# Cross attention one pair shorter in flight, the copy of the turned x ahead of the latent rows, the latent variance first in a pair, a second row of identity transposes

## The chip, the cores and the metric

One core of a Trainium2 chip runs the whole program in one launch. Time is the device time of one execution in microseconds (us); the runs of the kernel before gave 1091.06, 1090.47 and 1090.14, median 1090.47. The engines run their own instruction streams and meet at semaphores: PE (TensorE: matrix products, and transposes as products with the identity), DVE (VectorE), ACT (ScalarE), POOL (GpSimd) and SP (SyncE, which issues most transfers). Each engine takes its instructions in the order in which they are written.

## The reference

Three parts follow each other, each adding to x (32 sequences of 64 rows of 512 numbers): a masked cross attention over 256 context rows, a latent attention (q and kv are first projected to 384 + 128 + 64 columns, normalised and rotated), and a feed-forward part. The change lies in the first part and in the projection to latent rows:

```
x = x + xattn(layernorm(x), ctx, mask)          # scores = xn @ ctx.T, softmax, @ ctx
h = layernorm(x)                                # the "second normalisation"
z = h @ [wq_a; wkv_a].T + bias                  # 576 columns: q 384, kv 128, rope 64
q, kv = rmsnorm(z[:384]), rmsnorm(z[384:512])   # one mean of squares for each
rope = z[512:] * cos + rotate_half(z[512:]) * sin
```

## The kernel before

`stage_x` handles the 2048 rows as 16 pairs of sequences of 128 rows each. One slot of the loop (`slot(p, par)`, p = 0 to 15, written once for each engine) works on several pairs at once. In slot p of the kernel before:

- PE: `score(p)` (one product that adds the mask, then 16 of 64x256), `read(p-1)` (probabilities times context rows, 8 products), `turn1(p-2)` (4 transposes of the second normalisation), `turn0(p+1)`, `project(p-3)` (24 products of 288 columns with the latent weights), `turn` of the probabilities of p.
- ACT: copy of the turned probabilities of p-1 (L417), first normalisation of p+1 (L395, out x_xn), `squares(p-4)` (two sums of squares, L422 and L424), `exp(p)` (L412), `scale_q(p-4)` (L429), `turned1_hi(p-2)` (L406), `turned0(p+1)` (L400), second normalisation of p-1 (L395 too), and the transfer of z of pair p-4.
- DVE: `maximum(p)` (L503), `first_var(p+2)` (L467, L471, L474), `latent_var(p-4)` (two small instructions at L486 that wait for the sums of squares), `residual(p-1)` (L517, then L467, L471, L476), `turned1_lo(p-2)` (L462), `validate(p)` (L507, L512), `latent_kv(p-4)` (L491), `bias(p-3)` (L531, two).
- POOL: `rstd_of(0, p+2)` (L347, L351), `latent_rstd(p-4)` (L357), `rotate(p-4)` (L364 to L369), `rstd_of(1, p-1)` (L347, L351); in slot 2 also the rounding of the latent weights `w_raw` to `w_hi` (L381), from which DVE makes `w_lo` (L462).
- SP: the loads of x (p+6), of the turned context (p+4) and of the context rows (p+3), held back only by their buffers.

Whether a pair's second normalisation can start is set by a chain over three engines: `residual` and its variance on DVE, `rstd_of(1, ...)` on POOL, L395 on ACT. Behind slot 15 (the handover, in `program`) the last pairs are drained by hand-written lists while `Weights` multiplies the attention's weights out: 12 `fill_keys` (L1303) and then `fill_values` (L1313) on PE, each in one of four banks, which ACT (`keys_hi`, L1323) and DVE (`keys_lo`, L1338) empty, and `rope_scaled`, `rope_hi`, `rope_lo` on POOL (L1359, L1364, L1368).

Of the kernel before, what the change touches and what calls it, by code (L numbers as in the profile page):

```python
# [182 lines left out]
def stage_x(nc, ctx, A, scratch, mem, banks, w):  # L183
# [76 lines left out]
    def sync(sp):  # L260
# [66 lines left out]
        sp.dma_start(small[:], A["small"]).then_inc(s["small_loaded"], 16)  # L327
# [60 lines left out]
    def scalar(act):  # L388
# [42 lines left out]
        def slot(p, par):  # L431
# [130 lines left out]
    def tensor(pe):  # L562
        t = nc.tensor

        def turn(dst, src, n=KH):
# [28 lines left out]
        def score(p):  # L594
# [1520 lines left out]
```

## Time and profile before

| | |
|---|---|
| profiled execution | 1090.33 us, span 1088.5 us |
| busy | PE 1063.1 us (98%), PEld 904.0 (83%), DVE 508.1 (47%), ACT 338.9 (31%), POOL 294.9 (27%) |
| chain that ended last | PE 95%, DVE 2%, issue 1%, DMA 1%, POOL 1% |
| PE, 40 slices of 27 us | 5999989999999999999999999999999999999997 |
| GB/s in the first seven slices | 359 414 418 394 404 230 87 |
| waits of PE up to 230 us | 6.9 us for the first normalisation (L395), 3.7 us for `keys_lo` (L1338), 2.4 us for the turned probabilities (L417), 1.7 us for the mask (L557), 1.0 us for `turned0` (L400) |

PE is busy in all slices but the first, the sixth (the handover) and the last. A line of the timeline is one instruction, or several that merged: start, duration, engine, line, what it writes from what it reads, and in brackets how long the engine had been idle and what ended that. Durations overlap, since an engine starts the next instruction before the last has left its pipeline; the distance between two starts is what an instruction holds its engine.

### The profile page before, as it was taken

To read this page: it belongs to the slowest core of one execution; us is meant where nothing else is said; L and a number is where in the kernel's file an instruction comes from. 1 tells how busy PE (TensorE), PEld (TensorE's weight loads), DVE (VectorE), ACT (ScalarE), POOL (GpSimd) and SP (SyncE) were. 2 spreads that over 40 slices of the span, in tenths; PEclk is the share of its full clock that TensorE was granted. 3 is DMA by queue.
4 is the path that set the end of the run, shared out by engine and by line. 5 is a ranking of instruction groups with operands and counts; after the bars stand their busy time and mean duration, and the time that the engine had idled before them with its cause. 6 is when DMAs were issued, how large, how long until landed. Compare 5 with 4: busy or idle time off the path is not lost.

```text
span 1088.5 us, 18667 instructions
## 1 busy us (share of the span) xinstructions
PE 1063.1 (98%) x7233; PEld 904.0 (83%) x7233; DVE 508.1 (47%) x914; ACT 338.9 (31%) x630; POOL 294.9 (27%) x341
## 2 busy tenths in 40 slices
PE   5999989999999999999999999999999999999997
PEld 3677777788888888888888888999999898989896
DVE  3666556545555554445455668532324232414232
ACT  3565554422222222223222236312222221313030
POOL 2434363321112101131112102423233232415050
PEclk9999999999999999999999999999999999999999
DMA  9999962200022000320012072200101010101000
GB/s 359 414 418 394 404 230 87 74 20 21 20 68 88 20 19 14 107 58 20 20 59 88 20 252 90 77 20 20 39 1 40 1 39 0 39 0 40 1 21 20
DMA packets 40851, 101.26 MB, mean 93 GB/s; under 512 B 7049, under 2 KB 11172, under 8 KB 36292
## 3 DMA queue, kind: packets, MB, share of 16 engines
q1 hardware_dynamic: 39044, 96.62, 24.9%
q10 hardware_dynamic: 1728, 3.54, 0.8%
q8 instruction: 55, 0.90, 0.3%
q14 instruction: 24, 0.20, 0.1%
HBM read 74.45 MB, written 17.30 MB: 84 GB/s over the span
## 4 chain that ended last, share of the span: by engine, by line
PE 95%; DVE 2%; issue 1%; DMA 1%; POOL 1%; ACT 0%; SPq 0%; POOLq 0%; DVEq 0%; ACTq 0%
PE b_z L44 6%; PE b_z L46 6%; PE b_z L45 6%; PE b_score L44 5%; PE b_score L46 5%; PE b_prob L46 5%; PE b_score L45 5%; PE b_prob L44 5%; PE b_prob L45 5%; PE b_turn L44 4%; PE b_turn L46 4%; PE b_turn L45 4%; PE b_read L46 4%; PE b_read L44 4%; PE b_read L45 4%; PE b_read L619 2%
## 5 line engine op out<-in xcount | busy, mean ns | idle before, releaser
L1505 POOL TENSOR_TENSOR f_hT_lo<-f_h,f_hT_hi 128x512 fp32r<-128x512 f32 x64 | 92.4, 1444 | 106.2 <-ACT f_hT_hi L1550 96.9
L812 POOL TENSOR_TENSOR m_sc<-m_sc,m_rs 128x1024 f32<-128x1024 f32 x16 | 30.5, 1905 | 241.9 <-DVE m_rs L975 241.9
L1606 DVE TENSOR_TENSOR f_h<-f_h 128x512 f32<-128x512 f32 x64 | 49.7, 777 | 91.4 <-ACT f_h L1545 91.1
L44 PE MATMUL b_z<-m_zT_lo,m_wq_hi 128*128 128x512 f32 x192 | 75.0, 390 | 1.0 <-issue 0.7
L45 PE MATMUL b_z<-m_zT_hi,m_wq_lo 128*128 128x512 f32 x192 | 74.7, 389 | 0.0
L46 PE MATMUL b_z<-m_zT_hi,m_wq_hi 128*128 128x512 f32 x192 | 74.7, 389 | 0.0
L44 PE MATMUL b_turn<-f_xnT_lo,f_up_hi 128*128 128x256 f32 x256 | 72.6, 283 | 0.0
L44 PE MATMUL b_read<-f_xnT_lo,f_up_hi 128*128 128x256 f32 x256 | 72.5, 283 | 0.0
L45 PE MATMUL b_read<-f_xnT_hi,f_up_lo 128*128 128x256 f32 x256 | 72.4, 283 | 0.0
L46 PE MATMUL b_read<-f_xnT_hi,f_up_hi 128*128 128x256 f32 x256 | 72.4, 283 | 0.0
L46 PE MATMUL b_turn<-f_xnT_hi,f_up_hi 128*128 128x256 f32 x256 | 72.4, 283 | 0.0
L45 PE MATMUL b_turn<-f_xnT_hi,f_up_lo 128*128 128x256 f32 x256 | 72.4, 283 | 0.0
L983 DVE TENSOR_TENSOR m_x<-b_score,m_x 128x512 f32<-128x512 f32 x32 | 22.1, 690 | 95.8 <-PE b_score L46 95.8
L854 ACT ACTIVATE m_qT<-b_z,m_q_bias 128x512 f32<-128x512 f32 x64 | 44.0, 689 | 70.5 <-PE b_z L46 64.7
L802 POOL TENSOR_TENSOR m_qpe<-m_qpe,m_swapped 128x512 f32<-128x512 f32 x32 | 41.2, 1289 | 79.1 <-DMA m_swapped<-m_by_sin 79.1
L1550 ACT CAST f_hT_hi<-f_h 128x512 fp32r<-128x512 f32 x64 | 39.8, 622 | 57.3 <-DVE f_h L1606 57.3
L1545 ACT ACTIVATE f_h<-b_turn 128x512 f32<-128x512 f32 x32 | 19.1, 598 | 112.8 <-PE b_turn L46 112.8
L1487 POOL TENSOR_TENSOR f_ve<-f_mv,m_eps 128x2 f32<-128x2 f32 x15 | 3.4, 226 | 182.9 <-DVE f_mv L1580 182.9
L875 ACT ACTIVATE m_sc<-m_sc 128x512 f32<-128x512 f32 x32 | 20.2, 632 | 104.8 <-DVE m_sc L967 104.8
L44 PE MATMUL b_score<-m_wvo_lo,m_oT_hi 128*128 128x512 f32 x128 | 51.4, 401 | 0.0
L44 PE MATMUL b_score<-f_down_lo,f_hT_hi 128*128 128x512 f32 x128 | 50.5, 394 | 0.3 <-issue 0.3
L44 PE MATMUL b_prob<-m_wvo_lo,m_oT_hi 128*128 128x512 f32 x128 | 50.6, 395 | 0.0
(268 smaller groups left out, 3098.7 us busy)
## 6 DMA issues: line engine op xcount, KB each, us to landing
x_ctx_in<-ctx_rows_dram SPq DMA_DIRECT2D x16, 1024.0 KB, 15.0
x_ctxT<-ctx_turned_dram SPq DMA_DIRECT2D x15, 1024.0 KB, 14.9
m_swapped<-m_by_sin SPq DMA_DIRECT2D x128, 64.0 KB, 2.0
m_raw<-attn_raw_dram SPq DMA_DIRECT2D x6, 768.0 KB, 10.6
m_z_in<-z_scratch SPq DMA_DIRECT2D x4, 1152.0 KB, 5.7
x_x_all<-x_dram SPq DMA_DIRECT2D x16, 256.0 KB, 15.7
m_x<-x_scratch SPq DMA_DIRECT2D x4, 1024.0 KB, 6.0
x_scratch<-m_x SPq DMA_DIRECT2D x4, 1024.0 KB, 4.7
```

What stands on the lines that cost most here:

```text
L44: nc.tensor.matmul(out, lh, rl, start=first, stop=False)
L45: nc.tensor.matmul(out, ll, rh, start=False, stop=False)
L46: return nc.tensor.matmul(out, lh, rh, start=False, stop=last)
L619: mm = t.matmul(b_read[rows], pT[:, c, rows], ctx_in[:, p % RING, chunks * b + c], start=c == 0, stop=c == chunks - 1)
L802: q.tensor_tensor(qpe[:, m], qpe[:, m], swapped[:], ALU.add).then_inc(s["qpe_done"], 1)
L812: q.tensor_tensor(e, e, rs[:].unsqueeze(2).broadcast_to([P, HB, SEQ]), ALU.mult).then_inc(s["normed"], 1)
L854: a.activation(qT[:, h], b_q[h % 2][:], ACT.Identity, bias=q_bias[:, HU * n + h:HU * n + h + 1]).then_inc(s["q_done"], 1)
L875: a.activation(sc[:, HALF * half:HALF * half + HALF], sc[:, HALF * half:HALF * half + HALF], ACT.Exp, scale=SCALE).then_inc(s["exped"], 1)
L983: v.tensor_tensor(x1[:, TILES[i]], b_w[i % 2][:], x1[:, TILES[i]], ALU.add).then_inc(s["x2_done"], 1)
L1505: g.tensor_tensor(hT_lo[:, 2 * n:2 * n + 2].rearrange("p m n -> p (m n)"), h[:, n % 2], hT_hi[:, 2 * n:2 * n + 2].bitcast(F32).rearrange(" ...
L1550: a.copy(hT_hi[:, 2 * n:2 * n + 2].rearrange("p m n -> p (m n)"), h[:, n % 2]).then_inc(s["h_hi"], 1)
L1606: v.tensor_tensor(h[:, n % 2], h[:, n % 2], h[:, n % 2], ALU.mult).then_inc(s["squared"], 1)
```

## The change

Every pair is projected one slot earlier: `project`, `squares`, `latent_var`, `latent_rstd`, `rotate`, `scale_q`, `latent_kv`, `bias` and the transfer of z take p-2 or p-3 where they took p-3 or p-4, and the hand-written lists behind slot 15 lose one pair. On PE `turn1(p-2)` goes ahead of `read(p-1)`. On ACT `turned1_hi(p-2)` goes ahead of `exp(p)`, and `scale_q` behind `turned0`. On DVE `latent_var` becomes the first instruction of a slot and `turned1_lo(p-2)` goes ahead of `first_var(p+2)`. The rounding of the latent weights moves from POOL in slot 2 to ACT in slot 1, and their load ahead of the turned context of pair 2. Two rows of 22 identity transposes are issued on PE, one ahead of everything and one at the start of slot 2; nothing reads what they write. In pair 0 the mask is added behind the products instead of ahead of them. The two `rope_scaled` of POOL move from behind slot 15 to the starts of slots 14 and 15.

```diff
@@ -313,22 +314,22 @@
         sp.dma_start(mask_u8[:], A["mask_BxS2_bk0"]).then_inc(s["masks_loaded"], 16)
         sp.wait_ge(s["pool_setup"], 2)
         sp.dma_start(picks[0:BATCH, 0:PAIRS].rearrange("p a n -> p (a n)"), A["picks"]).then_inc(s["masks_loaded"], 16)
+        load_ctxT(1)
         load_x(2)
-        load_ctxT(1)
         load_ctx(0)
         load_x(3)
+        sp.dma_start(w_raw[:], A["w_latent"].rearrange("(k p) n -> p k n", p=P)).then_inc(s["w_loaded"], 16)
         load_ctxT(2)
+        load_x(4)
         load_ctx(1)
-        load_x(4)
-        sp.dma_start(w_raw[:], A["w_latent"].rearrange("(k p) n -> p k n", p=P)).then_inc(s["w_loaded"], 16)
+        sp.dma_start(small[:], A["small"]).then_inc(s["small_loaded"], 16)
         load_ctxT(3)
         load_ctx(2)
         load_x(5)
-        sp.dma_start(small[:], A["small"]).then_inc(s["small_loaded"], 16)
         slots(slot)
         return dict(store_z=store_z, store_x1=store_x1)
 
-    def gpsimd(pool):
+    def gpsimd(pool, rope_scaled):
         g = nc.gpsimd
         held = pool.alloc_register("x_pool_held")
         g.memset(ident[:], 0.0).then_inc(s["pool_setup"], 1)
...
@@ -369,16 +370,15 @@
             g.tensor_tensor(zbuf[:, par, QLR + KVLR:ZW], rope_tmp[:, 0, :], rope_tmp[:, 1, :], ALU.add).then_inc(s["z_rope"], 1)
 
         def slot(p, par):
+            if p >= PAIRS - w.ROPE_ROUNDS:
+                rope_scaled(p - (PAIRS - w.ROPE_ROUNDS))
             if has(p + 2):
                 rstd_of(0, p + 2)
-            if has(p - 4):
-                latent_rstd(p - 4)
-                rotate(p - 4, par)
+            if has(p - 3):
+                latent_rstd(p - 3)
+                rotate(p - 3, 1 - par)
             if has(p - 1):
                 rstd_of(1, p - 1)
-            if p == 2:
-                pool.wait_ge(s["w_loaded"], 16)
-                g.tensor_copy(w_hi[:], w_raw[:]).then_inc(s["w_hi"], 1)
 
         rstd_of(0, 0)
         rstd_of(0, 1)
...
@@ -433,19 +433,22 @@
                 turned_probs(p - 1)
             if has(p + 1):
                 norm(0, p + 1, xn0, x_all[:, p + 1])
-            if has(p - 4):
-                squares(p - 4, par)
-            exp(p)
-            if has(p - 4):
-                scale_q(p - 4, par)
+            if has(p - 3):
+                squares(p - 3, 1 - par)
             if has(p - 2):
                 turned1_hi(p - 2, par)
+            exp(p)
             if has(p + 1):
                 turned0(p + 1)
+            if has(p - 3):
+                scale_q(p - 3, 1 - par)
             if has(p - 1):
                 norm(1, p - 1, xn1, x_all[:, p - 1])
-            if has(p - 4):
-                write_z(act, p - 4, par)
+            if p == 1:
+                act.wait_ge(s["w_loaded"], 16)
+                a.copy(w_hi[:].rearrange(flat), w_raw[:].rearrange(flat)).then_inc(s["w_hi"], 1)
+            if has(p - 3):
+                write_z(act, p - 3, 1 - par)
 
         norm(0, 0, xn0, x_all[:, 0])
         turned0(0)
...
@@ -531,23 +534,23 @@
                 v.tensor_tensor(zb[:, par, cols], b_z[n][:, 0:ZH], qkv_b[:, cols], ALU.add).then_inc(s["z_biased"], 1)
 
         def slot(p, par):
+            if has(p - 3):
+                latent_var(p - 3)
             maximum(p)
+            if has(p - 2):
+                turned1_lo(p - 2, par)
             if has(p + 2):
                 first_var(p + 2)
-            if has(p - 4):
-                latent_var(p - 4)
             if has(p - 1):
                 residual(p - 1)
+            validate(p)
+            if has(p - 3):
+                latent_kv(p - 3, 1 - par)
             if has(p - 2):
-                turned1_lo(p - 2, par)
-            validate(p)
-            if has(p - 4):
-                latent_kv(p - 4, par)
-            if has(p - 3):
-                bias(p - 3, 1 - par)
+                bias(p - 2, par)
             if p == PAIRS - 3:
                 w.columns(dve)
-            if p == 2:
+            if p == 1:
                 dve.wait_ge(s["w_hi"], 1)
...
@@ -567,6 +570,10 @@
             for k in range(n):
                 last = t.transpose(dst[:, P * k:P * k + P], src[:, P * k:P * k + P], ident[:])
             return last
+
+        def warm():
+            for n in range(WARM):
+                t.transpose(banks.free[:, P * (n % 4):P * (n % 4) + P], ident[:], ident[:])
 
         def turn0(p):
             pe.wait_ge(s["norm0"], p + 1)
@@ -596,16 +603,18 @@
             pe.wait_ge(s["exped"], p)
             if p:
                 pe.wait_ge(s[f"ctxT_loaded{p % RING}"], 16 * (p // RING + (1 if p % RING else 0)))
-            if p == 0:
-                pe.wait_ge(s["masks_built"], 1)
-            t.matmul(b_score[:, 0:CTX], picks[:, p].bitcast(BF16), mask_rows, start=True, stop=False)
+            if p:
+                t.matmul(b_score[:, 0:CTX], picks[:, p].bitcast(BF16), mask_rows, start=True, stop=False)
             for k in range(KH):
                 if p == 0 and k % 2 == 0:
                     pe.wait_ge(s[f"ctxT_first{k // 2}"], 16)
                 for b in range(2):
                     rows = slice(SEQ * b, SEQ * b + SEQ)
                     mm = t.matmul(b_score[rows, 0:CTX], xnT0[:, k, rows], ctxT[:, p % RING, k, CTX * b:CTX * b + CTX],
-                                  start=False, stop=k == KH - 1)
+                                  start=p == 0 and k == 0, stop=p != 0 and k == KH - 1)
+            if p == 0:
+                pe.wait_ge(s["masks_built"], 1)
+                mm = t.matmul(b_score[:, 0:CTX], picks[:, p].bitcast(BF16), mask_rows, start=False, stop=True)
             mm.then_inc(s["scored"], 1)
 
         def read(p):
@@ -621,17 +630,22 @@
             mm.then_inc(s["read"], 1)
 
         def slot(p, par):
+            if p == 2:
+                warm()
+                turn1(p - 2)
             score(p)
+            if p == 2:
+                project(p - 2, par)
+            if p > 2:
+                turn1(p - 2)
             if has(p - 1):
                 read(p - 1)
             if p >= PAIRS - 2:
                 w.fill_bias(pe, HEADS // 2 * (p - PAIRS + 2), HEADS // 2 * (p - PAIRS + 3))
-            if has(p - 2):
-                turn1(p - 2)
             if has(p + 1):
                 turn0(p + 1)
-            if has(p - 3):
-                project(p - 3, 1 - par)
+            if p > 2:
+                project(p - 2, par)
             pe.wait_ge(s["exped"], p + 1)
             pe.wait_ge(s["pT"], p)
             turn(b_prob, probs, CTX // P).then_inc(s["p_turned"], 1)
@@ -639,6 +653,7 @@
                 w.turn_vectors(pe)
 
         pe.wait_ge(s["consts"], 3)
+        warm()
         turn0(0)
         slots(slot)
         return dict(read=read, project=project, turn1=turn1)
...
@@ -1778,21 +1792,17 @@
 
         @block.gpsimd
         def _(pool):
-            x, w = X["gpsimd"](pool), weights.gpsimd(pool)
-            m = M["gpsimd"](pool)
-            for n in range(weights.ROPE_ROUNDS):
-                w["rope_scaled"](n)
-            x["latent_rstd"](L - 3)
-            x["rotate"](L - 3, 1 - L % 2)
+            w = weights.gpsimd(pool)
+            x, m = X["gpsimd"](pool, w["rope_scaled"]), M["gpsimd"](pool)
             x["rstd_of"](1, L)
             x["latent_rstd"](L - 2)
             x["rotate"](L - 2, L % 2)
             w["rope_hi"](0)
+            w["rope_lo"](0)
             x["latent_rstd"](L - 1)
-            w["rope_lo"](0)
             x["rotate"](L - 1, 1 - L % 2)
+            w["rope_hi"](1)
             x["latent_rstd"](L)
-            w["rope_hi"](1)
             x["rotate"](L, L % 2)
             w["rope_lo"](1)
             m["groups"]()
```

Two places show the new order. On DVE, in a pair of the middle, before (x_x_all is x, xnT1b_lo the low part of the turned second normalisation, x_q_var the latent variance):

```order
L503 TENSOR_REDUCE x_negmax<-b_score 128x1
L467 BN_STATS x_stats_118<-x_x_all 128x6
L471 BN_AGGR x_mean_var_120<-x_stats_118 128x2
L474 TENSOR_SCALAR x_var_eps_122<-x_mean_var_120 128x1
L486 TENSOR_SCALAR x_q_var<-x_ssq 128x1 x2
L517 SCALAR_TENSOR_TENSOR x_x_all<-b_read,x_rvalid,x_x_all 128x512
L467 BN_STATS x_stats_119<-x_x_all 128x6
L471 BN_AGGR x_mean_var_121<-x_stats_119 128x2
L476 TENSOR_SCALAR x_var_eps_123<-x_mean_var_121 128x1
L462 TENSOR_TENSOR x_xnT1b_lo<-b_turn,x_xnT1b_hi 128x512
```

and now:

```order
L489 TENSOR_SCALAR x_q_var<-x_ssq 128x1 x2
L506 TENSOR_REDUCE x_negmax<-b_score 128x1
L465 TENSOR_TENSOR x_xnT1b_lo<-b_turn,x_xnT1b_hi 128x512
L470 BN_STATS x_stats_118<-x_x_all 128x6
L474 BN_AGGR x_mean_var_120<-x_stats_118 128x2
L477 TENSOR_SCALAR x_var_eps_122<-x_mean_var_120 128x1
L520 SCALAR_TENSOR_TENSOR x_x_all<-b_read,x_rvalid,x_x_all 128x512
L470 BN_STATS x_stats_119<-x_x_all 128x6
L474 BN_AGGR x_mean_var_121<-x_stats_119 128x2
L479 TENSOR_SCALAR x_var_eps_123<-x_mean_var_121 128x1
```

`x_q_var` and `xnT1b_lo` now stand ahead of the variance of the pair two ahead (x_stats_118) and of the residual; before, the one stood between the two and the other behind both. On ACT in slots 1 and 2, now (x_xn_104 is the first normalisation, x_xn_108 the second):

```order
L395 ACTIVATE x_xn_108<-x_x_all,x_shift_127,x_rstd_125 128x512
L449 CAST x_w_hi<-x_w_raw 128x2304
L417 COPY x_pT<-b_prob 128x256
L395 ACTIVATE x_xn_104<-x_x_all,x_shift_126,x_rstd_124 128x512
L406 CAST x_xnT1a_hi<-b_turn 128x512
L412 ACTIVATE x_probs,x_esum<-b_score,x_negmax 128x256
L400 COPY x_xnT_105<-b_turn 128x512
```

`x_w_hi` is new on ACT, behind pair 0's second normalisation and ahead of all that ACT does in slot 2; `xnT1a_hi` has passed the exponential.

## Rows read from the trace of the kernel before

**Rows 1.** Timeline, PE, a pair of the middle: start us, duration us, engine, line, what.

```profile
73.73 1.09 PE L568 MATMUL b_turn<-m_ident,x_xn 128*128 128x128 f32 x8
74.58 0.38 PE L44 MATMUL b_z<-x_w_lo,x_xnT1b_hi 128*128 128x288 f32 x1
...
78.05 0.27 PE L601 MATMUL b_score<-x_picks 128*128 128x256 bf16 x1
```

**Rows 2.** Timeline, ACT, the same pair.

```profile
69.51 0.81 ACT L395 ACTIVATE x_xn<-x_x_all,x_shift,x_rstd 128x512 f32<-128x512 f32 x1 [0.54 <-POOL x_shift L351]
70.23 0.37 ACT L417 COPY x_pT<-b_prob 128x256 f32<-128x256 f32 x1
70.50 0.81 ACT L395 ACTIVATE x_xn<-x_x_all,x_shift,x_rstd 128x512 f32<-128x512 f32 x1
...
77.63 0.81 ACT L395 ACTIVATE x_xn<-x_x_all,x_shift,x_rstd 128x512 f32<-128x512 f32 x1 [0.55 <-POOL x_shift L351]
```

**Rows 3.** Timeline, ACT, a pair of sums of squares.

```profile
157.14 0.51 ACT L422 ACTIVATE x_junk<-x_zb 128x384 f32<-128x384 f32 x1
...
157.99 0.19 ACT L424 ACTIVATION_READ_ACCUMULATOR x_junk<-x_zb 128x1 f32 x1
```

**Rows 4.** Timeline, DVE, behind them.

```profile
158.28 0.21 DVE L486 TENSOR_SCALAR x_q_var<-x_ssq 128x1 f32<-128x1 f32 x2 [0.26 <-ACT x_junk L424]
158.55 0.82 DVE L531 TENSOR_TENSOR x_zb<-b_z,x_small 128x288 f32<-128x288 f32 x2
159.41 3.51 DVE L491 SCALAR_TENSOR_TENSOR x_zbuf<-x_zb,x_q_rstd,x_small 128x128 f32<-128x128 f32 x1
```

**Rows 5.** Timeline, DVE, the pair of the middle.

```profile
68.51 0.69 DVE L462 TENSOR_TENSOR x_xnT1b_lo<-b_turn,x_xnT1b_hi 128x512 fp32r<-128x512 f32 x1 [0.74 <-ACT x_xnT1b_hi L406]
69.12 0.15 DVE L507 RECIPROCAL x_rinv<-x_esum 128x1 f32<-128x1 f32 x1
...
72.13 0.42 DVE L503 TENSOR_REDUCE x_negmax<-b_score 128x1 f32<-128x256 f32 x1 [1.64 <-PE b_score L607]
72.47 0.68 DVE L467 BATCH_NORM_STATS2 x_stats<-x_x_all 128x6 f32<-128x512 f32 x1
...
73.50 0.15 DVE L474 TENSOR_SCALAR x_var_eps<-x_mean_var 128x1 f32<-128x1 f32 x1
```

**Rows 6.** Timeline, POOL, the pair of the middle.

```profile
73.83 0.55 POOL L347 TENSOR_TENSOR x_rstd<-x_var_eps,m_neg_half 128x1 f32<-128x1 f32 x1 [4.36 <-DVE x_var_eps L474]
...
76.62 0.55 POOL L347 TENSOR_TENSOR x_rstd<-x_var_eps,m_neg_half 128x1 f32<-128x1 f32 x1
```

**Rows 7.** Timeline, SP, issue of pair 0's rows.

```profile
4.47 0.43 SPq L274 DMA_DIRECT2D x_ctx_in<-ctx_rows_dram  x1
```

**Rows 8.** DMA issues from 4.45 to 4.50 us: name, queue, KB, us to landing.

```profile
x_ctx_in<-ctx_rows_dram SPq DMA_DIRECT2D x1, 1024.0 KB, 10.2
```

**Rows 9.** Timeline, PE, the read product of pair 0.

```profile
17.07 1.89 PE L619 MATMUL b_read<-x_ctx_in,x_pT 128*64 128x512 f32 x8
```

**Rows 10.** Timeline, ACT, second normalisation of pair 0.

```profile
22.25 0.81 ACT L395 ACTIVATE x_xn<-x_x_all,x_shift,x_rstd 128x512 f32<-128x512 f32 x1 [2.08 <-POOL x_shift L351]
```

**Rows 11.** Groups by form, ACT: busy us, mean ns, idle before.

```profile
L1534 ACT CAST f_ex_hi<-f_ex_raw 128x2080 fp32r<-128x2080 f32 x1 | 1.9, 1932 | 1.0 <-PE b_prob L46 1.0
```

**Rows 12.** Timeline, DVE, the low part of the latent weights.

```profile
30.64 2.56 DVE L462 TENSOR_TENSOR x_w_lo<-x_w_raw,x_w_hi 128x2304 fp32r<-128x2304 f32 x1 [2.38 <-POOL x_w_hi L381]
```

**Rows 13.** Timeline, PE, pair 14's slot and the handover.

```profile
120.91 1.89 PE L619 MATMUL b_read<-x_ctx_in,x_pT 128*64 128x512 f32 x8
...
163.73 2.05 PE L1303 MATMUL b_free<-m_raw 128*128 128x128 f32 x8 [3.70 <-DVE m_wq_lo L1338]
...
174.77 0.49 PE L1042 MATMUL b_turn<-m_ident,m_z_in 128*128 128x128 f32 x3
```

**Rows 14.** Windows: stretch, us, busy by engine (x count), PEclk, DMA share, GB/s.

```profile
163.70:167.10 3.40, 3.37 (x17) 3.40 (x18) 2.48 (x6) 1.20 (x2) 1.53 (x3) 0.56 0.24 92
```

**Rows 15.** Timeline, POOL, beside the last of these.

```profile
159.34 3.43 POOL L1368 TENSOR_TENSOR m_wq_lo<-m_raw,m_wq_hi 128x1536 fp32r<-128x1536 f32 x1
```

More of the change, by code:

```diff
@@ L240, in stage_x @@
     XR = 6
+    WARM = 22
     QUERIES_AT = (11, 12, 12, 13, 13, 13)
@@ L1753, in _ @@
             x, m = X["sync"](sp), M["sync"](sp)
-            x["store_z"](L - 3, 1 - L % 2)
             x["store_x1"](L, 1, "x1_rest")
@@ L1809, in _ @@
             x["turned_probs"](L)
-            x["squares"](L - 3, 1 - L % 2)
+            w["keys_hi"](0)
+            x["squares"](L - 2, L % 2)
             x["turned1_hi"](L - 1, 1 - L % 2)
-            x["scale_q"](L - 3, 1 - L % 2)
-            w["keys_hi"](0)
+            x["scale_q"](L - 2, L % 2)
             w["keys_hi"](1)
+            w["keys_hi"](2)
             x["norm1"](L)
-            x["squares"](L - 2, L % 2)
             x["turned1_hi"](L, L % 2)
-            x["scale_q"](L - 2, L % 2)
-            w["keys_hi"](2)
+            x["squares"](L - 1, 1 - L % 2)
             w["keys_hi"](3)
             w["keys_hi"](4)
-            x["squares"](L - 1, 1 - L % 2)
             x["scale_q"](L - 1, 1 - L % 2)
-            for f in range(5, 9):
+            for f in range(5, 7):
                 w["keys_hi"](f)
             x["squares"](L, L % 2)
-            w["keys_hi"](9)
+            for f in range(7, 9):
+                w["keys_hi"](f)
             x["scale_q"](L, L % 2)
-            for f in range(10, weights.KEY_FILLS):
+            for f in range(9, weights.KEY_FILLS):
                 w["keys_hi"](f)
@@ L1880, in _ @@
             x, w, m = X["vector"](dve), weights.vector(dve), M["vector"](dve)
-            x["latent_var"](L - 3)
-            x["turned1_lo"](L - 1, 1 - L % 2)
-            x["latent_kv"](L - 3, 1 - L % 2)
-            x["bias"](L - 2, L % 2)
             w["bias"]()
             x["residual"](L)
+            x["turned1_lo"](L - 1, 1 - L % 2)
+            x["latent_var"](L - 2)
             w["keys_lo"](0)
+            x["latent_kv"](L - 2, L % 2)
             w["keys_lo"](1)
+            w["keys_lo"](2)
             x["bias"](L - 1, 1 - L % 2)
-            x["latent_var"](L - 2)
             x["turned1_lo"](L, L % 2)
-            x["latent_kv"](L - 2, L % 2)
-            w["keys_lo"](2)
+            x["latent_var"](L - 1)
             w["keys_lo"](3)
             w["keys_lo"](4)
-            x["latent_var"](L - 1)
+            x["latent_kv"](L - 1, 1 - L % 2)
             x["bias"](L, L % 2)
-            x["latent_kv"](L - 1, 1 - L % 2)
-            for f in range(5, 9):
+            for f in range(5, 7):
                 w["keys_lo"](f)
             x["latent_var"](L)
-            w["keys_lo"](9)
+            for f in range(7, 9):
+                w["keys_lo"](f)
             x["latent_kv"](L, L % 2)
-            for f in range(10, weights.KEY_FILLS):
+            for f in range(9, weights.KEY_FILLS):
                 w["keys_lo"](f)
@@ L1975, in _ @@
             x, w, m = X["tensor"](pe), weights.tensor(pe), M["tensor"](pe)
+            w["fill_keys"](0)
+            x["read"](L)
             x["turn1"](L - 1)
-            x["project"](L - 2, L % 2)
-            x["read"](L)
-            w["fill_keys"](0)
             w["fill_keys"](1)
+            w["fill_keys"](2)
             x["project"](L - 1, 1 - L % 2)
-            w["fill_keys"](2)
             x["turn1"](L)
             w["fill_keys"](3)
+            w["fill_keys"](4)
             x["project"](L, L % 2)
-            w["fill_keys"](4)
             w["fill_keys"](5)
```

## The prediction

> **What bounds the kernel now.** I read the page first: PE is busy for 98% of the span and carries 95% of the chain that ended last, so any time that the change brings or costs must appear as time in which PE waits, or is freed from waiting. The list of PE's waits puts all of the large ones ahead of 40 us and at the handover behind slot 15. Then I read one pair of the middle on every engine. PE has no gap in it; 78.05 - 74.58 = 3.5 us of it are the projection and the two transposes of the probabilities behind it, 3.2 without these [rows 1]. By ACT a pair takes 77.63 - 69.51 = 8.12 us [rows 2]. So in the middle PE sets the pace, and what decides there is whether another engine's chain from one pair to the next stays under 8.12 us.
>
> **The middle, where the sum is made.** In the changed order there is a chain that runs once around per pair and comes back to where it began. I follow it from the start of the second normalisation of pair q-1 on ACT to that of pair q, with the distance between starts where an engine does the next thing, and the time to the start of the waiting instruction where a semaphore lies between.
>
> - ACT, second normalisation of q-1 to the copy of the turned probabilities: 70.23 - 69.51 = 0.72. The copy: 70.50 - 70.23 = 0.27. The first normalisation behind it is the same instruction, 0.72 again [rows 2].
> - ACT, the two sums of squares, to the start of `latent_var` on DVE, which waits for them: 158.28 - 157.14 = 1.14 [rows 3, 4].
> - DVE, `latent_var`: 158.55 - 158.28 = 0.27 [rows 4]. It is now first in the slot, so `maximum` stands behind it, 72.47 - 72.13 = 0.34, and behind that `turned1_lo`, 69.12 - 68.51 = 0.61 [rows 5]. `turned1_hi`, for which that waits, is ready in time: ACT starts it right behind the squares and needs about as long as the two instructions ahead on DVE.
> - DVE, `first_var`, to the start of POOL's first rstd: 73.83 - 72.47 = 1.36 [rows 5, 6].
> - POOL, this rstd, the latent rstd and the rotation, to the rstd of pair q's second normalisation: 76.62 - 73.83 = 2.79 [rows 6]. `residual(q)` on DVE ends sooner than this, so POOL's queue decides, as it does now.
> - POOL to ACT's second normalisation of q: 77.63 - 76.62 = 1.01 [rows 2, 6].
>
> The sum is 0.72 + 0.27 + 0.72 + 1.14 + 0.27 + 0.34 + 0.61 + 1.36 + 2.79 + 1.01 = 9.23 us, 1.11 more than PE needs. Before, the ring does not close: `first_var` is released by `maximum`, which waits only for the scores, and the squares are needed only by `latent_var`, which stands behind it. Putting `latent_var` and `turned1_lo` ahead of `first_var` ties the POOL queue to ACT's squares, which stand behind the previous second normalisation. PE is held in it because `turn1(p-2)` now stands directly behind `score(p)` and waits for that normalisation, and the projection waits for the lower part that follows.
>
> The ring is whole wherever a slot has squares and a first variance, slots 3 to 13: eleven passes, from the second normalisation of pair 1 to that of pair 12. 11 x 9.23 = 101.5 us.
>
> **The head.** The rows of context of pair 0 land at 4.47 + 10.2 = 14.7 us [rows 7, 8]; the loads ahead of them are the same bytes in another order. Before, `read(0)` started only at 17.07 [rows 9], because the scores had waited for the mask and ran at the lower clock. With the mask last and the first row of transposes ahead it should start at 14.7. From there to the second normalisation of pair 0 it was 22.25 - 17.07 = 5.2 us [rows 9, 10], so 19.9. Until here 2.4 us are won.
>
> They are lost again behind it. The rounding of `w_raw` now stands on ACT behind this normalisation: 19.9 + 0.7 = 20.6. Its length on ACT isn't in the trace; a cast of 2080 columns takes 1.93 [rows 11], so 2304 take 2.1 (bounds: the 0.8 of a normalisation of 512 columns, and 2.6 as on DVE), to 22.7. The weights should have landed by 18.5, since 2.2 MB that stood ahead of them at about 410 GB/s do so no more. DVE makes `w_lo` in 2.56 [rows 12], to 25.3, and only then comes to `maximum(2)` and `turned1_lo(0)`: 0.34 + 0.69, so 26.3. The projection of pair 0 now stands ahead of `read(1)`: 3.2 us, to 29.5. `read(1)` to the second normalisation of pair 1, 5.2 again: 34.7. The second row of transposes lies in PE's wait for pair 0's normalisation and costs nothing: eight transposes hold PE for 74.58 - 73.73 = 0.85 us [rows 1], so 22 for 2.3, and they end before the normalisation does at 20.7. If that wait were gone they would cost these 2.3.
>
> The normalisation of pair 12 then starts at 34.7 + 101.5 = 136.2, and PE's `turn1(12)` at 137.0 behind its 0.8.
>
> **Slots 14 and 15 and the handover.** What PE does from there to the end of the eighth `fill_values` is what it did before from 120.91 (behind the scores of slot 14) to 174.77, less one projection: 53.9 - 3.2 [rows 13]. Before, it contained a wait of 3.70 us, and 3.4 us behind it at a granted share of 0.56 of the clock, 1.2 GHz in part, which lost (1 - 0.56) x 3.4 = 1.5 [rows 13, 14]. The wait was for `keys_lo`; ahead of it `latent_kv(15)` took 3.51 us on DVE beside POOL's `rope_lo`, 3.43 us [rows 4, 15]. Now `rope_lo(0)` comes ahead of the latent rstd of pair 14 and `rope_lo(1)` behind everything, so no `latent_kv` meets either, and the two `rope_scaled` lie in POOL's idle time ahead of slots 14 and 15. I take both losses as gone: 53.9 - 3.2 - 3.7 - 1.5 = 45.5, with up to 5.2 more if a new wait takes their place. 137.0 + 45.5 = 182.5, against 174.8: 7.7 us late. What follows is unchanged and bound by PE.
>
> So 1090.33 + 7.7 = 1098.0 for the profiled execution, and as it stood 0.14 under the median of the runs, 1098 for the median.
>
> **A rule on the clock.** The trace shows PE at 1.2 GHz behind an idle time of 3.70 us, and back at 2.4 GHz 3.4 us later [rows 13, 14]; what it did before that rise was products. The Trainium skill, "TensorE: Matmul & The Clock Gate", section "Part 4: PE-mode transpose", says that transposes do not count as activity for the clock gate. By that rule both rows of identity transposes would leave the clock where it is. No row here shows a rise behind transposes alone, so trace and rule don't contradict each other; the sum would be the one of the second rival below.
>
> **Rivals.**
>
> 1. The ring doesn't bind: a link in it is shorter than its pitch before, or hidden, and PE keeps its 8.12 us. Then from the normalisation of pair 1 at 34.7 `turn1(1)` starts at 35.6, `turn1(12)` at 35.6 + 11 x 8.12 = 124.9, and the eighth value fill ends at 124.9 + 45.5 = 170.4, 4.4 us early: 1086. For it: DVE and ACT are idle for 53% and 69% of the span. Against it: a ring of waits doesn't ask for shares, and each link is a queue order or a semaphore. It decides from a ring under 8.12 us, that is if 1.11 us of the sum fall away. Chance 0.15.
> 2. As forecast, and the clock stays low in the head: the scores of pair 0 take the time they took before, `read(0)` starts some 0.7 us later, and PE's wait of 3 us between the scores of pair 2 and the projection of pair 0 (23.3 to 26.3) lowers the clock for it, at 1.5 us as in the handover: 1098 + 2.2 = 1100. Against it: the wait is shorter than the 3.70 of before. Chance 0.13.
> 3. The ring binds by half, at 8.6 us, because ACT reaches the squares sooner than I reckon in some slots: 11 x 0.6 us less, 1091. Chance 0.10.
>
> **How the numbers follow.** My forecast has 0.62, with its own range 1094 to 1102: 0.2 us on the ring makes 2.2, the head is good to 2, the handover may hold a new wait. The range to quote reaches to the first rival's time, 1086 to 1102, and leaves out what lies beyond it. A measurement of this kernel tells 0.2%, 2.2 us, from no change. Faster: the first rival and the lower edge of the third, 0.18. Within 2.2 us: the middle of the third, 0.05. Slower: 0.77.
>
> **What would show it.** In the trace after, second normalisations of consecutive pairs from pair 1 to pair 12 stand about 9.2 us apart on ACT, DVE waits for the squares at the head of every slot, and PE has two short waits in each, about 0.5 us each, for the second normalisation and for `turned1_lo`. `read(0)` starts near 14.7, the first projection near 26.3, pair 1's second normalisation near 34.7. The handover has no wait of 3 us and no low clock. The prediction is wrong if pairs stand 8.1 us apart, or if the first projection comes before 24 or behind 29 us.

## The result, and the profile after

The changed kernel takes 1099.49 us (median of 4 runs, 1098.42 to 1099.58) against 1090.47 before: ratio 1.0082, 95% interval 1.0068 to 1.0097. It is 9.0 us slower; 7.5 were forecast. The profiled execution took 1099.49 us. Of the page after: span, busy shares, PE in 40 slices, GB/s, and the chain that ended last.

```profile
span 1097.6 us, 18756 instructions
PE 1075.4 (98%) x7277; PEld 909.0 (83%) x7277; DVE 504.5 (46%) x914; ACT 341.3 (31%) x631; POOL 292.4 (27%) x340
PE   7999999999999999999999999999999999999997
GB/s 360 416 357 306 333 369 132 80 26 21 11 67 97 15 16 21 68 96 20 18 51 97 20 210 127 78 1 39 20 21 39 1 38 0 38 0 39 1 20 20
PE 86%; DVE 4%; POOL 3%; issue 3%; ACT 2%; DMA 1%; ACTq 0%; POOLq 0%; DVEq 0%
```

The shares hide the loss: PE is busy for 98% as before, and shows less of a gap in the first slice and none in the sixth. What tells is the last line. PE's part of the chain has fallen from 95% to 86%; DVE, POOL and ACT have come into it. The transfers of the fourth to sixth slices show 306 to 369 GB/s where they showed 394, 404 and 230: pairs pass more slowly, and the loads run on longer.

One pair of the middle. ACT, where 72.93 and 82.00 are second normalisations and 73.91 a first one, answering to [rows 2, 3]:

```profile
72.93 0.81 ACT L395 ACTIVATE x_xn<-x_x_all,x_shift,x_rstd 128x512 f32<-128x512 f32 x1 [1.50 <-POOL x_shift L352]
...
73.65 0.35 ACT L417 COPY x_pT<-b_prob 128x256 f32<-128x256 f32 x1
73.91 0.81 ACT L395 ACTIVATE x_xn<-x_x_all,x_shift,x_rstd 128x512 f32<-128x512 f32 x1
74.62 0.51 ACT L422 ACTIVATE x_junk<-x_zb 128x384 f32<-128x384 f32 x1
...
82.00 0.81 ACT L395 ACTIVATE x_xn<-x_x_all,x_shift,x_rstd 128x512 f32<-128x512 f32 x1 [1.50 <-POOL x_shift L352]
```

DVE behind it, answering to [rows 4, 5]:

```profile
75.76 0.21 DVE L489 TENSOR_SCALAR x_q_var<-x_ssq 128x1 f32<-128x1 f32 x2 [3.39 <-ACT x_junk L424]
75.90 0.42 DVE L506 TENSOR_REDUCE x_negmax<-b_score 128x1 f32<-128x256 f32 x1
76.24 0.68 DVE L465 TENSOR_TENSOR x_xnT1b_lo<-b_turn,x_xnT1b_hi 128x512 fp32r<-128x512 f32 x1
76.84 0.68 DVE L470 BATCH_NORM_STATS2 x_stats<-x_x_all 128x6 f32<-128x512 f32 x1
```

POOL, with the start of the rotation between, answering to [rows 6]:

```profile
78.20 0.55 POOL L348 TENSOR_TENSOR x_rstd<-x_var_eps,m_neg_half 128x1 f32<-128x1 f32 x1 [5.30 <-DVE x_var_eps L477]
...
79.82 0.32 POOL L365 TENSOR_TENSOR x_rope_tmp<-x_zb,x_small 128x64 f32<-128x64 f32 x1
...
80.98 0.55 POOL L348 TENSOR_TENSOR x_rstd<-x_var_eps,m_neg_half 128x1 f32<-128x1 f32 x1
```

The ring is there and closes in 82.00 - 72.93 = 9.07 us. Each bracket names the next member: ACT waits for POOL, DVE for ACT's sums of squares at the head of the pair, POOL for DVE. Its links, by starts: 0.72 + 0.26 + 0.71 + 1.14 + 0.14 + 0.34 + 0.60 + 1.36 + 2.78 + 1.02 = 9.07.

The head on PE:

```profile
1.53 4.76 PE L576 MATMUL b_free<-m_ident 128*128 128x128 f32 x22 [1.53 <-POOL m_ident L339]
...
8.20 1.95 PE L613 MATMUL b_score<-x_ctxT,x_xnT 128*64 128x256 f32 x16 [0.68 <-ACT x_xnT L400]
...
14.78 1.94 PE L628 MATMUL b_read<-x_ctx_in,x_pT 128*64 128x512 f32 x8 [0.67 <-issue]
...
17.36 2.56 PE L576 MATMUL b_free<-m_ident 128*128 128x128 f32 x22
...
26.39 0.60 PE L44 MATMUL b_z<-x_w_lo,x_xnT1a_hi 128*128 128x288 f32 x1 [2.88 <-DVE x_xnT1a_lo L465]
...
31.31 1.94 PE L628 MATMUL b_read<-x_ctx_in,x_pT 128*64 128x512 f32 x8
```

`read(0)` starts at 14.78 (14.7 forecast), the first projection at 26.39 (26.3). But the projection lasts until 31.31, 4.9 us instead of 3.2. Windows of the same trace (columns as in [rows 14]), the second one the stretch of the handover that stood at 0.56:

```profile
26.40:29.80 3.40, 3.40 (x14) 3.40 (x15) 0.87 (x3) 0.00 (x0) 0.81 (x2) 0.50 1.01 410
...
163.70:167.10 3.40, 3.13 (x27) 2.90 (x26) 2.83 (x5) 2.62 (x7) 3.32 (x3) 1.00 0.65 194
```

Behind its wait of 2.88 us PE ran at a granted 0.50, 1.2 GHz. The handover has neither the wait nor the low clock: from 137 to 184 us the granted clock is 1.00 throughout. From `turn1(12)` at 137.72 to the end of the eighth value fill at 183.66 it takes 45.9 us (45.5 forecast). DVE's three `latent_kv` in it take 0.41, 0.41 and 0.34 us, and none stands beside a `rope_lo` of POOL (those start at 165.25 and 176.63). The first of them:

```profile
162.56 0.41 DVE L494 SCALAR_TENSOR_TENSOR x_zbuf<-x_zb,x_q_rstd,x_small 128x128 f32<-128x128 f32 x1 [0.46 <-POOL x_q_rstd L358]
```

### The profile page after: what moved, and what is told of

Same layout as the page of the kernel before. It is cut to its first block, busy times and chain, and to the rows that moved or that the text cites. A ratio compares the mean times of both kernels' runs of the same rounds, so it can differ in the third digit from the quotient of the medians.

```text
span 1097.6 us, 18756 instructions
## 1 busy us (share of the span) xinstructions
PE 1075.4 (98%) x7277; PEld 909.0 (83%) x7277; DVE 504.5 (46%) x914; ACT 341.3 (31%) x631; POOL 292.4 (27%) x340
## 4 chain that ended last, share of the span: by engine, by line
PE 86%; DVE 4%; POOL 3%; issue 3%; ACT 2%; DMA 1%; ACTq 0%; POOLq 0%; DVEq 0%
PE b_z L44 6%; PE b_z L45 5%; PE b_z L46 5%; PE b_score L44 5%; PE b_score L46 5%; PE b_prob L46 5%; PE b_prob L44 5%; PE b_score L45 5%; PE b_prob L45 5%; PE b_turn L44 4%; PE b_turn L46 4%; PE b_turn L45 4%; PE b_read L46 4%; PE b_read L44 4%; PE b_read L45 4%
```

## Experiments on the ring

**e1_first_var_second.** The changed kernel with DVE's slot as `maximum`, `first_var`, `latent_var`, `turned1_lo`:

```diff
-            latent_var(p - 3); maximum(p); turned1_lo(p - 2, par); first_var(p + 2)
+            maximum(p); first_var(p + 2); latent_var(p - 3); turned1_lo(p - 2, par)
```

> The changed kernel (1099.5 us) with one edit on DVE: first_var(p+2) back directly behind maximum(p), and latent_var(p-3) and turned1_lo(p-2) behind it. Ring theory: the ring over ACT's squares, DVE and POOL is cut, PE sets the pace again at 8.12 us a pair instead of 9.07. Pair 1's second normalisation stays at 36.5 us, so turn1(12) starts at 36.5 + 0.9 + 11 x 8.12 = 126.7 instead of 137.7: 11.0 us less, 1088.5 us. Rival (the pairs are longer because the projection one slot earlier leaves PE waiting whatever DVE's order is): pairs stay near 9.1 us, 1099.5 us. Second rival (the squares don't matter, only POOL's queue): 9.1 as well.

Measured: 1093.86 us (1092.61 to 1095.48), ratio to before 1.0028 (1.0019 to 1.0038). The slope changed in the way expected: pairs 8.43 us apart and PE without a wait, so the ring no longer binds. PE in that pair:

```profile
79.29 0.27 PE L607 MATMUL b_score<-x_picks 128*128 128x256 bf16 x1
79.49 1.95 PE L613 MATMUL b_score<-x_ctxT,x_xnT 128*64 128x256 f32 x16
81.37 0.66 PE L571 MATMUL b_turn<-m_ident,x_xn 128*128 128x128 f32 x4
81.96 1.94 PE L628 MATMUL b_read<-x_ctx_in,x_pT 128*64 128x512 f32 x8
83.83 0.66 PE L571 MATMUL b_turn<-m_ident,x_xn 128*128 128x128 f32 x4
...
87.72 0.27 PE L607 MATMUL b_score<-x_picks 128*128 128x256 bf16 x1
```

The time missed by 5.4 us, all of it ahead of `turn1(12)`: from there to the eighth value fill this run takes 45.9 us too. First, PE by itself needs 8.43 us for a pair and not 8.12 (87.72 - 79.29). From `turn1(1)` at 38.97 to `turn1(12)` at 132.21 it takes 93.2 us, where 11 x 8.12 = 89.3 were expected: 3.9. Second, the second normalisation of pair 1 started at 38.10 instead of 36.54: 1.6. `turned1_lo(0)` came 0.9 us later behind `first_var(4)`, PE's wait for it grew to 3.99 us, and the whole projection behind it ran at the lower clock, 5.6 us (27.26 to 32.87).

**e2_latent_var_behind, e3_lo_behind.** One of the two instructions each behind `first_var`:

```diff
-            latent_var(p - 3); maximum(p); turned1_lo(p - 2, par); first_var(p + 2)
+ e2:        maximum(p); turned1_lo(p - 2, par); first_var(p + 2); latent_var(p - 3)
+ e3:        latent_var(p - 3); maximum(p); first_var(p + 2); turned1_lo(p - 2, par)
```

> The changed kernel with latent_var(p-3) alone moved behind first_var(p+2); turned1_lo stays ahead of it. Ring theory: turned1_lo still waits for turned1_hi, which stands behind the squares on ACT, so the ring stays closed and loses only what latent_var added: turned1_hi ends 0.09 us ahead of the end of maximum, 8.98 us a pair instead of 9.07, 11 x 0.09 = 1.0 us less, 1098.5 us. Rival (the wait of latent_var at the head of the slot is the cause by itself): 8.12 us a pair, 1088.5 us.

> The changed kernel with turned1_lo(p-2) alone moved behind first_var(p+2); latent_var stays first. Ring theory: the ring stays closed through latent_var and maximum and loses turned1_lo's 0.60 us: 8.47 us a pair, 11 x 0.60 = 6.6 us less, 1092.9 us. Rival (turned1_lo ahead of first_var is the cause by itself): 8.12 us a pair, 1088.5 us. If neither order matters: 1099.5 us.

Measured: e2 1098.71 us (1098.25 to 1099.10), pairs 8.99 apart; e3 1097.71 (1096.12 to 1098.17), pairs 8.55 apart. Second normalisations of e3 on ACT, one of a pair and one of the next:

```profile
80.40 0.81 ACT L395 ACTIVATE x_xn<-x_x_all,x_shift,x_rstd 128x512 f32<-128x512 f32 x1 [1.50 <-POOL x_shift L352]
...
88.95 0.81 ACT L395 ACTIVATE x_xn<-x_x_all,x_shift,x_rstd 128x512 f32<-128x512 f32 x1 [1.58 <-POOL x_shift L352]
```

Both agree with the ring: without `latent_var` it still runs over `turned1_hi`, which waits on ACT behind the squares (8.99 for 8.98), and without `turned1_lo` it is shorter by about that instruction's pitch (8.55 for 8.47). The time of e3 missed its mark by 4.8 us. In its trace `turn1(12)` starts at 134.62, 3.1 us earlier than in the changed kernel (137.72) and not 6.6: pair 1 came 1.1 us late, for the reason as in e1, and the eleven passes on PE took 96.1 us (38.49 to 134.62) instead of 93.7. Behind `turn1(12)` it takes 45.9 us again. The profiled execution, 1096.12, is 1.6 us below the median of its runs; that part of the miss no trace shows.

**e9_rotate_last.** The changed kernel, only POOL's slot altered:

```diff
                 latent_rstd(p - 3)
-                rotate(p - 3, 1 - par)
             if has(p - 1):
                 rstd_of(1, p - 1)
+            if has(p - 3):
+                rotate(p - 3, 1 - par)
```

> The changed kernel with the rotation of pair p-3 behind the rstd of the second normalisation of pair p-1 on POOL, instead of ahead of it; no other engine is touched. Theory (the ring of waits runs through POOL's queue): the four instructions of the rotation, 80.98 - 79.82 = 1.16 us in the changed kernel's trace, leave the ring. The second rstd then waits for DVE, which has its input at about 80.0, so the ring takes 9.07 - 0.9 = 8.2 us and PE's own 8.43 decide: pairs 8.43 us apart without waits on PE, 11 x 0.64 = 7.0 us less, 1092.5. Rival (the POOL queue is beside the ring, the residual on DVE or PE's order holds the pairs apart): pairs stay at 9.07, 1099.5.

Measured: 1099.73 us (1099.46 to 1100.07), ratio 1.0081 (1.0064 to 1.0098): nothing gained. By the time alone the rival would have won. The rows tell otherwise. POOL's second rstd, then ACT (ACTq is the issue of the transfer of z):

```profile
79.82 0.54 POOL L348 TENSOR_TENSOR x_rstd<-x_var_eps,m_neg_half 128x1 f32<-128x1 f32 x1 [0.33 <-DVE x_var_eps L480]
...
81.65 0.32 POOL L370 TENSOR_TENSOR x_zbuf<-x_rope_tmp 128x64 f32<-128x64 f32 x1
```

```profile
80.84 0.81 ACT L396 ACTIVATE x_xn<-x_x_all,x_shift,x_rstd 128x512 f32<-128x512 f32 x1 [0.69 <-POOL x_shift L352]
82.04 0.34 ACTq L259 DMA_DIRECT2D z_scratch<-x_zbuf  x1
82.48 0.37 ACT L418 COPY x_pT<-b_prob 128x256 f32<-128x256 f32 x1 [0.82 <-POOL x_zbuf L370]
82.75 0.81 ACT L396 ACTIVATE x_xn<-x_x_all,x_shift,x_rstd 128x512 f32<-128x512 f32 x1
...
90.03 0.81 ACT L396 ACTIVATE x_xn<-x_x_all,x_shift,x_rstd 128x512 f32<-128x512 f32 x1 [0.69 <-POOL x_shift L352]
```

From POOL's first rstd (77.85 there) to the second it is now 1.97 us instead of 2.78, and POOL waits there for DVE: the link is 0.8 shorter. But ACT issues the transfer of z behind the second normalisation, and this waits for the rotation. The copy of the turned probabilities comes 82.48 - 80.84 = 1.64 us behind the normalisation instead of 0.72. The ring closes in 90.03 - 80.84 = 9.19 us. That eleven longer passes end in the same time has to do with the head: in this trace the clock stayed up behind PE's wait of 2.31 us, and the second normalisation of pair 1 started at 35.64 instead of 36.54. A wait was moved from POOL's queue into ACT's, in the same ring; my expectation had left the transfer out.

## Experiments on PE's order

**e7_before_turn1_ahead.** The kernel before, `turn1(p-2)` directly behind `score(p)`:

```diff
             score(p)
+            if has(p - 2):
+                turn1(p - 2)
             if has(p - 1):
                 read(p - 1)
...
-            if has(p - 2):
-                turn1(p - 2)
```

> The kernel before (1090.5 us) with one edit on PE: turn1(p-2) directly behind score(p), ahead of read(p-1). Theory from the run with first_var second, where PE took 8.43 us a pair without a wait: PE pays about 0.15 us at each change between products of 64 and of 128 columns of the array, and splitting the eight transposes adds two changes: 8.12 + 0.31 = 8.43 us a pair in slots 2 to 15, 11 to 14 x 0.31 = 3.4 to 4.3 us more, 1094.4 us. Rival (the 0.31 us came from the shorter pipeline, its semaphores or its transfers): 1090.5 us, 8.12 us a pair.

Measured: 1094.92 us (1093.31 to 1095.90), ratio 1.0041 (1.0026 to 1.0055); pairs 8.43 us apart and no wait. The order by itself makes PE's pair as long as it was in e1.

**e10_before_mask_last.** The kernel before, in every pair the mask's product behind the scores instead of ahead (in pair 0 the wait for the mask moves with it); the eight transposes stay together:

```diff
-            t.matmul(b_score[:, 0:CTX], picks[:, p].bitcast(BF16), mask_rows, start=True, stop=False)
...
-                                  start=False, stop=k == KH - 1)
+                                  start=k == 0, stop=False)
+            mm = t.matmul(b_score[:, 0:CTX], picks[:, p].bitcast(BF16), mask_rows, start=False, stop=True)
```

> The kernel before, with the mask's product (128 columns of weights) behind the 16 products of the scores (64 columns) in every pair, so that PE changes between 128 and 64 columns four times in a pair instead of twice; the transposes stay a block of eight. Theory (a change of the width costs PE time; it is what made the pair 8.43 instead of 8.12 us when four transposes stood between scores and read): pairs about 8.4 us apart, 16 x 0.31 = 5 us more, about 1095. Rival (what costs is that the eight transposes are split in two groups of four): pairs stay at 8.12 us and the time at 1090.5, or below it by up to 1.7 us, since the mask of pair 0 is waited for later.

Measured: 1092.35 us (1091.49 to 1093.58), ratio 1.0012 (1.0002 to 1.0022). PE, one pair:

```profile
78.48 1.95 PE L604 MATMUL b_score<-x_ctxT,x_xnT 128*64 128x256 f32 x16
80.36 0.28 PE L608 MATMUL b_score<-x_picks 128*128 128x256 bf16 x1
80.57 1.94 PE L619 MATMUL b_read<-x_ctx_in,x_pT 128*64 128x512 f32 x8
...
86.85 1.95 PE L604 MATMUL b_score<-x_ctxT,x_xnT 128*64 128x256 f32 x16
```

A pair takes 86.85 - 78.48 = 8.37 us with the same instructions and four changes of width instead of two: 0.25 more for two changes. So the width is what costs, and splitting the transposes can hold 0.06 of the 0.31 at most. The time rose by less than expected, since the first pairs, in which PE waits anyway, cost nothing, and the later mask wins there: the second normalisation of pair 4 starts at 52.70, 0.6 us earlier than before. From there to the eighth value fill it takes 2.8 us more, and that fill ends 2.2 us later (177.00 against 174.77). The Trainium skill, "TensorEngine Tiling (Array Packing)", section "Key Properties", says that changing the tiling mode drains the engine. The runs agree in that a change costs time, and give the price: 0.13 us for one by this run, 0.16 by e7.

## Experiments on the head

Three runs change one of the rows of transposes in the changed kernel: **e5_row_behind_scores** puts the second behind the scores of pair 2, **e12_no_second_row** leaves it out, **e6_no_first_row** leaves out the first.

```diff
             if p == 2:
-                warm()              # e5, e12
                 turn1(p - 2)
             score(p)
             if p == 2:
+                warm()              # e5
                 project(p - 2, par)
...
-        warm()                      # e6
         turn0(0)
```

> The changed kernel (1099.5 us) with the second row of 22 identity transposes moved behind the scores of pair 2, so that it fills 2.4 of the 2.9 us for which PE waits ahead of the first projection. Clock theory: that wait lowers the clock at 26.4 us and the first projection takes 4.9 us instead of 3.2; filled, the clock stays at 2.4 GHz, pair 1's second normalisation starts at 34.9 instead of 36.5 and everything behind it 1.6 earlier: 1097.9 us. Rival (transposes don't count for the clock, as the rule has it, and the row only shifts the time of the fall): 1099.5 us.

> The changed kernel without the first row of transposes. If transposes raise the clock: it rises at about 13 us as in the kernel before, the first turn takes 1.1 instead of 0.66 us and the scores of pair 0 3.4 instead of 1.95, read(0) starts some 0.7 us later (15.5), second normalisation of pair 0 at 20.7. Rival (they don't): the clock rises near 6 us all the same and nothing moves.

> The changed kernel without its second row of 22 transposes, at the start of slot 2. Theory (the row lies in a wait of PE and is free; what it does is keep the clock): PE is idle from 17.4 to about 20.9 us, its clock falls, the scores of pair 2 take 1.7 us longer and end at about 25.3, still ahead of the lower part of pair 0 at 26.3 for which the projection waits; the time stays, 1099.5 within 0.5. If the clock is up again by 26.3, the projection of pair 0 gains the 1.7 us that it lost to the low clock in the changed kernel: 1098. Rival (the row keeps the clock for the projection too): 1101.

Measured: e5 1099.93 us (1099.05 to 1100.56); e6 1099.12 (one run); e12 1097.92 (1097.38 to 1098.72), ratio 1.0066 (1.0050 to 1.0083). PE in e12:

```profile
21.06 0.96 PE L571 MATMUL b_turn<-m_ident,x_xn 128*128 128x128 f32 x4 [3.34 <-ACT x_xn L395]
...
22.16 3.17 PE L613 MATMUL b_score<-x_ctxT,x_xnT 128*64 128x256 f32 x16
...
26.59 0.40 PE L44 MATMUL b_z<-x_w_lo,x_xnT1a_hi 128*128 128x288 f32 x1 [1.25 <-DVE x_xnT1a_lo L465]
...
29.95 1.94 PE L628 MATMUL b_read<-x_ctx_in,x_pT 128*64 128x512 f32 x8
```

Without the row PE idles for 3.34 us and the clock falls for the scores of pair 2. They take 3.17 instead of 1.95 us, but behind them PE waits for the lower part anyway, and the wait shrinks to 1.25. The clock is back by 26.6, and the projection takes 3.4 us, not 4.9, the case that the expectation gave 1098. In the changed kernel's trace the second row kept the clock where it was worth nothing, and it fell where it cost 1.7. The second normalisation of pair 1 starts at 35.18 in e12 and 36.54 in the changed kernel, and the eighth value fill ends 1.4 us earlier. The medians differ by as much (1.6), though the intervals of the two ratios overlap. It is no fixed price either: e6 and e9 have the second row too, and there the clock did not fall ahead of the projection, which took 3.4 us. e5 kept the clock in the projection, but its row ran from 25.80 to 28.83 and held the projection up instead; my expectation had the wait for the normalisation (3.35 us, low clock behind it) left out.

e6, PE:

```profile
6.89 1.09 PE L571 MATMUL b_turn<-m_ident,x_xn 128*128 128x128 f32 x4 [6.89 <-ACT x_xn L395]
8.65 3.68 PE L613 MATMUL b_score<-x_ctxT,x_xnT 128*64 128x256 f32 x16 [0.68 <-ACT x_xnT L400]
...
16.24 1.89 PE L628 MATMUL b_read<-x_ctx_in,x_pT 128*64 128x512 f32 x8
```

and two windows of e6, the wait ahead of the first projection, and the projection:

```profile
24.90:27.70 2.80, 0.03 (x2) 0.00 (x0) 2.80 (x4) 1.30 (x4) 0.00 (x0) 1.00 1.02 424
27.80:31.00 3.20, 3.19 (x24) 3.19 (x24) 0.89 (x3) 0.00 (x0) 0.82 (x2) 1.00 1.03 403
```

Without the first row the scores of pair 0 take 3.68 us at the lower clock instead of 1.95, and `read(0)` starts at 16.24 instead of 14.78. So a row of transposes alone does bring the clock up, and the other traces agree: without the first row the scores of pair 0 take 3.44 to 3.68 us (the kernel before, e4, e6, e7, e10), with it 1.95 to 2.06, but for e8. The profile's clock column is no help there: it stands at 1.00 until its first recorded fall, in the kernel before also beside scores of 3.44 us. So the start is told by durations. Here the wait of 2.9 us ahead of the projection was not followed by a low clock, and by pair 1 the two kernels are level (36.41 and 36.54). What the first row won, the low clock in the projection took.

**e8_both** joins the edits of e1 and e5.

> The changed kernel with first_var behind maximum (1093.9 us by itself) and the second row of transposes behind the scores of pair 2. There the clock was low for 6.8 us in the head and the first projection ended 1.6 us later than in the changed kernel. Clock theory: filled, pair 1's second normalisation starts at 34.9 instead of 38.1 and pairs of 8.43 us follow: 1090.7 us. Rival (the row doesn't hold the clock): 1093.9 us.

Measured: 1092.67 us (1092.05 to 1093.45), ratio 1.0018 (1.0009 to 1.0028): the best form of the shorter pipeline that I ran, still behind the kernel before. It missed its mark by 2.0 us, and so did pair 1's second normalisation (36.88, 34.9 expected). The clock did hold in the projection, 3.4 us from 28.28. But `turned1_lo(0)` started at 27.54, 1.0 us later than in e1, and the scores of pair 0 ran at the lower clock although the first row stood ahead of them. PE and its window:

```profile
8.20 3.61 PE L613 MATMUL b_score<-x_ctxT,x_xnT 128*64 128x256 f32 x16 [0.68 <-ACT x_xnT L400]
8.20:11.70 3.50, 3.50 (x16) 1.72 (x16) 0.28 (x1) 0.81 (x1) 0.82 (x2) 0.51 1.01 380
```

## Experiments on the handover

**e4_before_rope_lo_ahead** is the kernel before with `rope_lo(0)` ahead of the latent rstd of pair 14. **e11_before_head_and_handover** adds the first row of transposes and the mask last in pair 0.

```diff
+            w["rope_lo"](0)
             x["latent_rstd"](L - 1)
-            w["rope_lo"](0)
             x["rotate"](L - 1, 1 - L % 2)
```

> The kernel before (1090.5 us) with one edit on POOL behind slot 15: rope_lo(0) ahead of the latent rstd of pair 14, so that no latent_kv stands beside it. Theory of the handover: latent_kv of pair 14 takes 0.35 us instead of 3.51, PE's wait of 3.70 us for keys_lo shrinks to about 0.5 and the low clock behind it (1.5 us) doesn't come: 4.7 us less, 1085.8 us. Rival (the wait comes from ACT's squares and scale_q ahead of the keys, and the long latent_kv only fills it): 1090.5 us.

> The kernel before with three parts of the change that lie outside the ring: the first row of 22 transposes, the mask behind the products in pair 0, and rope_lo(0) ahead of the latent rstd of pair 14 on POOL (in addition to the earlier run of this last part alone, 1088.2). Theory (the head of the kernel before is held by the turned context or the rows of pair 2 that land near 30 us, so an earlier read(0) is lost there): between 1087 and 1088, taken 1087.3. Rival (read(0) 2.4 us earlier carries through to the middle): 1088.2 - 2.4 = 1085.8.

Measured: e4 1088.20 us (1086.94 to 1088.71), ratio 0.9973 (0.9962 to 0.9983); e11 1087.50 (1085.70 to 1089.83), ratio 0.997 (0.996 to 0.998). Both beat both kernels. PE's waits behind 100 us in e4:

```profile
PE b_free L1303 <- DVE m_wq_lo L1338: 1.5, 1, 1.5
PE b_score L1313 <- DVE m_wq_lo L1338: 0.7, 1, 0.7
```

The 3.70 us and the low clock behind them [rows 13, 14] are gone by this one line, since no `latent_kv` stands beside `rope_lo` any more: that of pair 14 takes 0.40 us instead of 3.51. But 2.2 us of waits for `keys_lo` are left, and only about half of the expected gain came. In e11 the head starts earlier and gains nothing, as PE then meets the load of the turned context of pair 3:

```profile
27.61 0.37 PE L604 MATMUL b_score<-x_picks 128*128 128x256 bf16 x1 [3.23 <-DMA x_ctxT<-ctx_turned_dram]
27.90 3.68 PE L610 MATMUL b_score<-x_ctxT,x_xnT 128*64 128x256 f32 x16
```

The second normalisation of pair 0 starts at 20.08 instead of 22.25 [rows 10]; the 2.2 us became a wait of 3.23 us and a low clock. So the head of the kernel before has its loads close behind, and an earlier start alone wins nothing. The difference of e11 to e4 is below what these runs tell.

## Why the prediction was right, and where not

- **The ring** was the main cause, and its size was near: 9.07 against 9.23 us. The link that was off is `latent_var` to `maximum`, 0.14 and not 0.27 (before, a wide `bias` stood behind it). Eleven passes took 136.86 - 36.54 = 100.3 us, 101.5 forecast. e1, e2 and e3 cut or shorten it where the links say; e1 gives back 5.6 of the 9.0 us, although its head was 1.6 us later. e9 shows that it runs over POOL's queue and that the sum is right only with every instruction that ACT issues; the first rival, no ring, is out. One sentence on it was too strong: that the ring does not close before. A shorter one does close there, from the squares over `latent_var` straight to POOL's latent rstd, without `first_var`. By the rows of the kernel before it is 0.72 + 0.27 + 0.72 + 1.14 + 0.39 + 1.85 + 1.01 = 6.1 us (0.39 from `latent_var` at 158.28 to the latent rstd at 158.67, 1.85 from the latent rstd at 74.77 to 76.62); it lies under PE's 8.12 and hides. The change made this ring longer.
- **PE's own pair** was mis-sized: I took 8.12 us for the changed order, and it is 8.43. It cost little here, since the ring hides it in the pairs of the middle; only slots 14 and 15 pay 0.31 each. It means that cutting the ring gives 0.64 us a pair and not the 1.11 I had, and that the first rival's 1086 was out of reach even without a ring: e1 stands at 1093.86. PE's two waits in a pair are therefore 0.3 us each and not 0.5, by distances of starts: `score` to `turn1` 2.19 (73.80 - 71.61 there, 1.88 in e1).
- **The head** came 1.8 us late at pair 1 (36.54, 34.7 forecast). The step that was mis-sized is the 3.2 us of the first projection: behind PE's wait it ran at 1.2 GHz and took 4.9. That is half of the second rival. Its other half, that transposes leave the clock low, is refuted by e6 against the changed kernel. By its number, 1100, that rival is nearer to the measured 1099.5 than the forecast of 1098; the 1.5 us between are mostly this term.
- **The second row** was forecast as free. Its own 2.6 us are; but through the clock it cost about 1.4 in the changed kernel's trace (against e12).
- **The handover**: 45.9 us against 45.5. Both losses of before went (the `latent_kv` of 3.51 us was that of pair 14, not 15 as I wrote; it changes nothing); e4 shows that `rope_lo` beside `latent_kv` made them, and that its move is worth 2.4 us without anything else of the change.

Summed up at the eighth value fill: 183.66 - 182.5 = 1.2 us over the forecast, from +1.8 (head), -1.2 (ring) and +0.5 (behind the normalisation of pair 12, where slots 14 and 15 pay for the width). So the mechanism was right, but that the sum came out this close is in part luck: a ring reckoned too long made up for most of a head reckoned too short. What stays open is when the clock falls, as the last point below shows.

## What to carry to other kernels

When an instruction is moved ahead in an in-order queue, look for the ring that it closes: follow each release until it comes back to its start, count every instruction issued on the way (transfers too), and compare the sum with the pitch of the bounding engine; shares of busy time say nothing on it. Before tuning a head or a handover, ask what stands behind it: time won ahead of a load or of a wait is paid back, and a low clock is free where the engine would wait anyway. Keep matrix products of one width together.

## What the runs showed of the hardware

- A change between products of 128 and of 64 columns costs PE 0.13 to 0.16 us: 8.12 us a pair with two changes, 8.37 (e10) and 8.43 (e7) with four.
- Transposes with the identity raise the clock. The 22 at the start take 4.76 us and the 22 later ones 2.56, and the four that follow the first row take 0.66 us, 1.09 where it is left out (e6). In the prediction I had cited the Trainium skill, "TensorE: Matmul & The Clock Gate", section "Part 4: PE-mode transpose", for the contrary; for these fp32 transposes the measurement decides against it.
- The length of a wait alone does not tell whether the clock falls. Waits of PE of 3.2 to 4.0 us, at 17 us or later, were always followed by 1.2 GHz, at once or within about 1 us (e1, e3, e5, e7, e8, e10, e11, e12, [rows 13, 14]). Of three waits of 2.88 us one was followed by it at once (the changed kernel), one about 1 us into the projection (e2) and one not at all (e6), nor was the 2.31 us of e9. And in e8 the four transposes behind the first row took 0.66 us, so the clock was up; yet the scores that followed ran at a granted 0.51, and PE had waited no longer than 1.15 and 0.68 us.
